# A graph layer on one core: the mixing branch's first product for two tiles at once, and five gather slots

## The reference

```python
xn = layernorm(x)
x = x + gnn(xn, edges) + mix(xn)          # gnn: softmax over each node's edges, weighted sum of rows
x = x + ffn(layernorm(x))                 # eight experts, three products each, gates by a softmax
# mix, per node:
h = relu(batchnorm(logmap0(xn) @ w_qkv))  # 256 -> 768 channels: the product of this change
s = w_pw(w_dw * h)                        # 768 -> 768, beside h itself
q, k, v = ...                             # 512 each, from cat(h, s)
out = relu(q) * sum(relu(k)) * v / (v + eps)   # per group of 32
mix = w_res(out) + b_res                  # with norms clipped in between
```

## Time and profile before

| | |
|---|---|
| median of 3 runs | 1184.98 us (1182.02 to 1188.89) |
| the profiled execution | 1176.66 us |
| its span | 1174.9 us |
| busy PE / DVE / ACT / POOL | 83% / 67% / 45% / 32% |
| PE passes (matmul records) | 5483, with as many weight loads |
| mean granted clock of PE | 0.923 |

### The profile page before, as it was taken

How to read it: one execution, slowest core, us unless ns; L and a number is a source line. 1 busy time by engine, 2 the same in 40 slices (tenths; PEclk the granted TensorE clock), 3 DMA queues, 4 the chain that set the end, 5 groups by cost and what they waited for, 6 DMA issues and landing times.

```text
span 1174.9 us, 15618 instructions
## 1 busy us (share of the span) xinstructions
PE 973.4 (83%) x5483; PEld 838.3 (71%) x5483; DVE 787.9 (67%) x1394; ACT 529.1 (45%) x1088; POOL 380.3 (32%) x408
## 2 busy tenths in 40 slices
PE   0998477878878888888764558999999999999996
PEld 0776356766767767766653447889978899998986
DVE  6786557777877977879787874676555454554544
ACT  1200034444444444444432135656655666667663
POOL 0034755666666666666676500000000000000000
PEclk9997779999998898999977777999999999999999
DMA  7332433434334343443447410000000000000012
GB/s 208 115 88 73 135 97 112 115 105 118 109 112 122 102 121 98 117 118 106 116 117 214 140 51 5 1 1 1 16 13 1 28 21 8 27 1 1 1 37 74
DMA packets 51375, 89.39 MB, mean 76 GB/s; under 512 B 10454, under 2 KB 34346, under 8 KB 51277
## 3 DMA queue, kind: packets, MB, share of 16 engines
q0 software_dynamic: 18768, 52.88, 16.6%
q1 hardware_dynamic: 32509, 35.27, 9.5%
HBM read 81.42 MB, written 6.68 MB: 75 GB/s over the span
## 4 chain that ended last, share of the span: by engine, by line
PE 55%; DVE 20%; issue 12%; ACT 6%; another core or an unknown queue 4%; DVEq 1%; DMA 1%; SPq 0%; ACTq 0%; POOL 0%; POOLq 0%
PE bank L872 12%; PE bank L873 11%; PE bank L874 11%; PE bank L750 5%; DVE U L1310 4%; DVE G L1202 3%; PE bank L788 3%; PE bank L680 2%; PE bank L709 2%; PE bank L799 2%; ACT junk L490 2%; PE bank L813 2%; DVE oh L1190 1%; PE bank L939 1%
## 5 line engine op out<-in xcount | busy, mean ns | idle before, releaser
L428 POOL DMA_INDIRECT G<-projected_rows,src_l x391 | 376.9, 964 | 288.9 <-issue 106.6
L750 PE MATMUL bank<-G,oh 128*128 128x264 f32 x782 | 201.9, 409 | 73.4 <-issue 38.9
L1473 DVE TENSOR_TENSOR hil<-hid,hil 128x1024 fp32r<-128x1024 f32 (+2 forms) x112 | 121.9, 1089 | 201.8 <-ACT hil L621 201.7
L750 PEld LDWEIGHTS bank<-G,oh 128*128 128x128 f32 x782 | 153.3, 201 | 111.4 <-issue 51.3
L613 ACT ACTIVATE hid<-bank,faff 128x512 f32<-128x512 f32 (+2 forms) x224 | 158.9, 722 | 151.6 <-PE bank L874 149.6
L872 PE MATMUL bank<-ew,hil 128*128 128x256 f32 (+1 forms) x400 | 113.5, 284 | 1.5 <-DVE feat_rows L1485 1.5
L873 PE MATMUL bank<-ew,hil 128*128 128x256 f32 (+1 forms) x400 | 113.0, 283 | 0.0
L874 PE MATMUL bank<-ew,hil 128*128 128x256 f32 (+1 forms) x400 | 113.0, 282 | 0.0
L621 ACT CAST hil<-hid 128x1024 fp32r<-128x1024 f32 (+2 forms) x112 | 105.3, 940 | 9.8 <-ACT hid L613 0.4
L1202 DVE TENSOR_TENSOR G<-G,bank 128x3072 f32<-128x3072 f32 (+1 forms) x33 | 109.0, 3304 | 0.0
L788 PEld LDWEIGHTS bank<-feat_rows,wqkv 128*128 128x128 f32 x600 | 82.6, 210 | 20.1 <-ACT TT L504 12.0
(11 more groups left out here) (289 smaller groups left out, 1656.4 us busy)
## 6 DMA issues: line engine op xcount, KB each, us to landing
dstb<-targets SPq DMA_DIRECT2D x32, 384.0 KB
G<-projected_rows,src_l POOLq DMA_INDIRECT x391
projected_rows<-sums SPq DMA_DIRECT2D x25, 132.0 KB, 3.6
x_in<-in_x SPq DMA_DIRECT2D x3, 1024.0 KB, 8.3
U<-in_x SPq DMA_DIRECT2D x24, 128.0 KB
out<-feat_rows SPq DMA_DIRECT2D x24, 128.0 KB
TT<-in_W SPq DMA_DIRECT2D x8, 256.0 KB
wqkv<-in_W SPq DMA_DIRECT2D x8, 256.0 KB
```

The source lines that it names most:

```text
L428: g.indirect_dma_start(out=G[slot][:, c, :], out_offset=None, in_=table[:, :], in_offset=bass.IndirectOffsetOnAxis(ap=src_l[:, grp, c:c + ...
L750: ins = T.matmul(b_seg[g % 2][:, 0:ROW], oh[g % 2][:, c, :], G[g % SLOTS][:, c, :], start=(c == 0), stop=(c == ch - 1))
L1473: V.tensor_tensor(hidl[layer][par][:, :, 0:cols], hid[layer][:, :, 0:cols], hidh[layer][par][:, :, 0:cols].bitcast(F32), ALU.subtract).the ...
```

## The change

The first product of the mixing branch is taken for a pair of tiles. A round is two chunks of 128 channels (4 matmuls of up to 256 columns) and fills `b_z`; three rounds make a pair, 13 pairs make 39 rounds (the last pair is one tile). Rounds are spread over two iterations: in an iteration with even t one early and one late round, with odd t only one early; in the iteration before tile 0 all three of the first pair, one early and two late. ACT normalises a round with two instructions of 256 columns and sets one semaphore, `z_evac`; the next round waits for it. u_rows takes its half of the pair's buffer. A pair's `TT` needs twice the columns of a tile; there are two such buffers, and the second one lies where the sixth gather slot was, so there are five slots.

```diff
-SLOTS = 6
+SLOTS = 5
+ROUNDS = 3 * -(-NT // 2)
...
+        tt_odd = sb("TT_odd", [P, EC * ROW])
...
-        TT = [tt_all[:, i * MC * P:(i + 1) * MC * P].rearrange("p (c n) -> p c n", c=MC) for i in range(2)]
+        TT = [b[:, 0:2 * MC * P].rearrange("p (c n) -> p c n", c=MC) for b in (tt_all, tt_odd)]
...
+        def rounds_of(t):
+
+            if t == -1:
+                return (0,), (1, 2)
+            first_ = 3 * (t // 2 + 1)
+            both = ((first_,), (first_ + 1,)) if t % 2 == 0 else ((first_ + 2,), ())
+            return tuple(tuple(r for r in slot if r < ROUNDS) for slot in both)
+
+        def round_of(r):
+
+            pair, part = divmod(r, 3)
+            start = 2 * pair * P
+            return pair, range(2 * part, 2 * part + 2), start, min(2 * P, NPAD - start)
...
-                    sp.wait_ge(s["zb_mm"], NT)
+                    sp.wait_ge(s["z_mm"], ROUNDS)
...
-            def batch_norm(t, chunks):
-                act.wait_ge(s["za_mm" if chunks[0] == 0 else "zb_mm"], t + 1)
-                for c in chunks:
-                    ins = A.activation(TT[t % 2][:, c, :], b_z[:, c % 4 * P:(c % 4 + 1) * P], ACT.Relu,
+            def batch_norm(r):
+                pair, chunks, _, cols = round_of(r)
+                act.wait_ge(s["z_mm"], r + 1)
+                for i, c in enumerate(chunks):
+                    ins = A.activation(TT[pair % 2][:, c, 0:cols], b_z[:, i * 256:i * 256 + cols], ACT.Relu,
                                        bias=baff[:, 1, c:c + 1], scale=baff[:, 0, c:c + 1])
-                ins.then_inc(s["bna_done" if chunks[0] == 0 else "tt_ready"], 1)
+                ins.then_inc(s["z_evac"], 1)
...
-            def channels(t, cs):
-                if cs[0] == 0:
+            def channels(r):
+                _, chunks, start, cols = round_of(r)
+                if r == 0:
                     pe.wait_ge(s["baff_ready"], 1)
-                    need(pe, s["tt_ready"], t)
-                    done = s["za_mm"]
-                else:
-                    pe.wait_ge(s["bna_done"], t + 1)
-                    done = s["zb_mm"]
-                for c in cs:
+                need(pe, s["z_evac"], r)
+                for i, c in enumerate(chunks):
                     for k in range(KC):
-                        ins = T.matmul(b_z[:, c % 4 * P:(c % 4 + 1) * P], wqkv[:, k, c * P:(c + 1) * P], FM[:, k, t * P:(t + 1) * P],
+                        ins = T.matmul(b_z[:, i * 256:i * 256 + cols], wqkv[:, k, c * P:(c + 1) * P], FM[:, k, start:start + cols],
                                        start=(k == 0), stop=(k == KC - 1))
-                ins.then_inc(done, 1)
+                ins.then_inc(s["z_mm"], 1)
 
             def u_rows(t):
-                pe.wait_ge(s["tt_ready"], t + 1)
+                pe.wait_ge(s["z_evac"], 3 * (t // 2 + 1))
...
-                        ins = T.matmul(bank[m][:, h * 256:(h + 1) * 256], TT[t % 2][:, c, :], ip[:, 0:c + 2:c + 1, :], start=True, stop=True)
+                        ins = T.matmul(bank[m][:, h * 256:(h + 1) * 256], TT[t // 2 % 2][:, c, t % 2 * P:(t % 2 + 1) * P], ip[:, 0:c + 2:c + 1, :], start=True, stop=True)
...
-                if 0 <= t + 1 < NT:
-                    channels(t + 1, range(0, 4))
+                early_rounds, late_rounds = rounds_of(t) if -1 <= t < NT else ((), ())
+                for r in early_rounds:
+                    channels(r)
```

More of the change, by code:

```diff
@@ L127, in program @@
             ew_all = late_sb("ew", 2 * 2 * 3 * KC * F)
-            late_sb("under_slots", SLOTS * EC * ROW - 2 * KC * NPAD - 2 * 2 * 3 * KC * F, F32)
+            late_sb("under_slots", (SLOTS + 1) * EC * ROW - 2 * KC * NPAD - 2 * 2 * 3 * KC * F, F32)
             hid_all = [late_sb(f"hid{i}", KC * MAXB, F32) for i in range(2)]
@@ L263, in program @@
             "sw_mm prod_ready var_mm baff_ready acc_init",
-            "za_mm zb_mm bna_done tt_ready u_mm u_evac fsq_ready qk_ready eps_ready",
+            "z_mm z_evac u_mm u_evac fsq_ready qk_ready eps_ready",
             "o_ready o_tr oT_ready r_mm mixed_ready no2_ready",
@@ L545, in _ @@
                     epsilon(t)
-                if 0 <= t + 1 < NT:
-                    batch_norm(t + 1, range(0, 4))
+                early_rounds, late_rounds = rounds_of(t) if -1 <= t < NT else ((), ())
+                for r in early_rounds:
+                    batch_norm(r)
                 if 0 <= t - 1 < NT:
                     mixed_out(t - 1)
-                if 0 <= t + 1 < NT:
-                    batch_norm(t + 1, range(4, MC))
+                for r in late_rounds:
+                    batch_norm(r)
                 if g == NA + MIX0 + 1:
@@ L838, in _ @@
                     mixed_out(t - 1)
-                if 0 <= t + 1 < NT:
-                    channels(t + 1, range(4, MC))
+                for r in late_rounds:
+                    channels(r)
             pe.wait_ge(s["mx_tr"], 1)
```

## The result

The change takes the kernel from 1183.5 us (median of 4, 1178.48 to 1188.89) to **1170.42 us** (median of 4, 1167.79 to 1172.42) on the same chip (the median of before has one run more than in the table ahead of the prediction). The ratio is 0.9889, its 95% interval 0.9852 to 0.9926: faster by 1.1%, 13 us. The forecast was 1164 us with a range of 1146 to 1198. The profiled execution took 1172.42 us (span 1170.5), against 1176.66 (1174.9) before.

The account below looks back on a forecast made before the run. In the main loop, PE stalls were taken to hold up DVE above its 16.2 us per iteration. Relief of 21 us and about 0 elsewhere took the profiled 1176.66 to about 1156, plus 8.3 to the median: 1164 us, range 1146 to 1198.

Parts of the forecast that it names:

- The bound and what there was to win: Main loop, 160 to 615 us: DVE's own 16.2 us per iteration is the bound; 41 us could be won.
- The excess of 41 us: DVE's wait at its once-per-tile reduction: 60.4 us, less 19.5 us that clean iterations have too.
- The gaps: -21 us: Main loop: fewer PE instructions relieve the stalls, -21 us, the middle between 5.7 and all 41.
- the proportional 5.7: Lower end of the main loop's relief: excess shrinks only with PE's instruction count, 0.14 x 41 = 5.7 us.
- The expected sign: Profile after: PE's "issue" before L750 and L813 well under 53 us.
- Array time, ACT, order: 0: Main loop: 2 us less array time, 20 us less ACT work and the new round order, each booked at 0.
- (d): Even iterations: the long late round meets the stall, slower, 1200 to 1212 us; 0.20 with weaker forms (1190 to 1212).
- The start: +4.5 - 4: Before tile 0: making the whole first pair loses 4.5 us, a shorter L750 crawl regains 4; about 0.
- (b): Main loop: relief only proportional, -5.7 + 4.5 - 2, about 1182 us; chance 0.13.
- the offset: Whole kernel: the median lies 8.3 us above the profiled execution, taking about 1156 to 1164 us.
- (a): PE's loop: gaps are the price of two branches between L750 and L813, which stay; 1187 us, chance 0.13.
- (c): Whole kernel: stalls belong to recording the profile and go from the profiled execution alone; timed 1187 us, chance 0.08.

Follow-up runs that it names:

- experiment 8: The kernel before with 6 of 12 gathers per group from the seventh group on: 1117.78 us and 1118.07 us, ratio 1.0 both times, on chips without gaps.
- experiment 4: The kernel before without PE's two branches and their register loads in each iteration: 1187.0 us, ratio 1.0006.
- experiment 1: The changed kernel, unaltered, on another chip: 1118.23 us against 1118.13 of the kernel before there, ratio 1.0002.

## Why the prediction held, point by point

**The bound and what there was to win.** Right. The reading of the clean iterations, 16.2 us under the gaps, is what the chips without gaps do in 17 of 24 intervals. The excess of 41 us was the right size too: on these chips the loop takes 43 us less (440.1 - 397.4, the second of after, since before has no profile there), and it was put down to the gaps. What makes the gaps it left open, and so do the runs.

**The gaps: -21 us.** Right in kind, near in size: the loop gave 18.7 in the two profiles. The value came from the middle between the proportional 5.7 and all 41, which is a choice and no working, so that it came so near is in part luck. That the count of instructions is behind it is supported by three loops: after with twelve small matmuls 441.8, after with the products split 437.1, after with one wide matmul 426.5. The expected sign, "issue" before L750 and L813 well under 53 us, came (3.5 us), but it was a bad sign: 28.3 us of it had moved to L757. PE's gaps in all fell by 12 us only, and DVE's idle time in the loop by 18.9. Why DVE gains more than PE's gaps lose is not worked out by any row; the gap at L757 ahead of the next group's score rows can lie beside DVE's own work, which fits, and was not tested.

**Array time, ACT, order: 0.** Right where there are no gaps: the 288 passes more of the split version cost nothing there. The array's time itself was sized low: in the two windows of experiment 8 PE is busy for 344.95 us with before's products and 339.47 with after's, 5.5 us and not 2. Where there are gaps, the split version's loop (437.1 against 445.9 on the same chip) leaves room for some us of the rounds and of ACT's steps, from one profile each. ACT's normalisations, 55.5 us for 144, are 72 of 35.9 us in after: 19.6 us less against 20 in the forecast, and no late step of an iteration was seen to wait for it. Rival (d), the long round that meets a stall, did not come as a whole: where L803 ran its 8 passes in one piece in the loop they took 1.89 or 1.99 us, and the intervals got shorter. In a few rounds gaps broke the eight up (6.7 us in 7 gaps).

**The start: +4.5 - 4.** Right in its sum and not in its path: the first reduction starts at 160.47 us, before at 160.48. Order of time in after, PE and ACT at tile 0:

```profile
121.47 1.97 PE L803 MATMUL bank<-feat_rows,wqkv 128*128 128x256 f32 x8
...
132.18 0.38 PE L768 MATMUL bank<-G,oh 128*128 128x264 f32 x1 [0.33 <-issue]
...
147.59 1.02 ACT L521 ACTIVATE TT<-bank,baff 128x256 f32<-128x256 f32 x2 [13.62 <-remote]
148.66 3.78 PE L803 MATMUL bank<-feat_rows,wqkv 128*128 128x256 f32 x8 [16.10 <-ACT TT L521]
...
153.55 1.99 PE L803 MATMUL bank<-feat_rows,wqkv 128*128 128x256 f32 x8 [1.11 <-ACT TT L521]
155.38 0.45 PE L757 MATMUL bank<-hsel,ohT 128*128 128x24 bf16 x12
```

From the late part to L757 it takes 155.38 - 148.66 = 6.7 us, before 152.80 - 150.93 = 1.87: 4.9 lost, inside the 4.3 to 6.1. Of these, 150.93 - 148.66 = 2.3 us come back ahead of it and the rest behind it. The crawl of L750 up to 150.93 is gone; PE has done with it at 132.56, 18 us earlier. But ACT then stands 13.62 us before the normalisation of a product that was ready at 121.47 + 1.97 us, and takes nearly all of it back. On chip 4 the same normalisation starts at 131.88 right behind the exponentials of 131.61, and the first reduction at 148.6. So that stand is no dependency of the program. It looks like the same disturbance on the next engine, and the relief of PE's crawl brought no more than 2.3 us.

**What the sum lacked: the rest after the last tile, +14.** The prediction priced the stretch from 160 to 615 us, and let the end move along with it. This is the term that it lacked: 14.3 of the 18.7 us gained in the loop were given back next to 17 unbroken gathers. After with the twelve small matmuls, where the loop gains nothing, has before's rest of 574.3 us. In total the change won 13 us by the medians, between the forecast's -21 and rival (b)'s -3.

**From the profiled execution to the median.** The sum was made at 1156 and set 8.3 us higher, as before's profiled execution stood under its median. After's stands 2.0 above (1172.42 and 1170.42). The miss by the sum is 1172.4 - 1156 = 16 us, of which 14.3 are the tail and 2.3 the smaller relief; the offset hid 10.3 of it. The 6 us between 1164 and 1170.42 are small because two errors oppose each other, which is luck. Two smaller slips: rivals (a) and (b) are priced with +4.5 for the start and -2 for the passes where the forecast books both at about 0, and the upper end of the range, 1198, is called the lower part of (d), which by its own sum begins at 1200.

**The rivals.** (a) was refuted by experiment 4. The Trainium skill, "Runtime: NRT & Kernel Launch", section "Instruction fetch mechanics", says that a taken branch whose target lies outside the prefetched pages stalls the engine for a fetch; in this kernel removing them from PE's loop changed nothing (1.0006), so here it was no part of the time. Whether these targets lie outside those pages no run here shows. (b) has the sign and not the size. (c), that the gaps are in the profiled execution alone, is refuted as it was put: the timed runs got faster by 1.1% where the profile shows gaps and by nothing where it shows none, and before is 65 us slower there in its timed runs too. In a wider form it stands, and it is the strongest rival left: every timed run here lists a span and a granted clock, as a recorded one does, and records of landings are missing just where the gaps are (experiment 1). If the gaps hang on recording, so do the 13 us. (d) did not happen.

**What stays open.** Which path backs up. That it clears when the gathers pause fits the tail (after 613.51, all engines go on at 616.71 to 617.75) and the start (the row of POOL's gathers ends at 143.28 us, ACT goes on at 147.59), but in no run on a chip with gaps were the gathers fewer. Fewer gathers would also mean fewer records of landings (6417 in place of 8923 on chip 4), so that run alone would not tell gathers from records; one that records nothing would. Why some chips show the gaps and others not is open too. And whether a pause in the tail could bring back the 14 us there: with its price of 13 us, hardly in the form tried. After itself was not run beside its variants on chips 8 and 10, so that its comparison with them may go across chips, and no version was faster than after on a chip with gaps.

## What to carry to other kernels

When several engines stand still together in mid-series, with "issue" or an unknown releaser, run the kernel on a second chip before anything is priced, and look whether the trace is whole: here that one look split the time into 1118 us that the kernel needs and 65 that came on some chips only, together with missing records, and showed that the change works on the second part alone. Merging narrow matmuls into wider ones seems to relieve such gaps through the number of instructions, and was worth nothing where another engine set the pace (1.0002). And a gain in one stage needs a line in the sum for the next stage: compare the time from the stage's last row to the end, before and after.

## What the runs showed of the hardware

- The same kernel takes 1118 us on two chips (2 and 4) and 1183 to 1187 us on others (8, 10 and that of the result), with the same instructions. Whether that is the chip or its surroundings at that time was not separated. The difference lies in the start (11.9 us), the loop (24.0 us for after; for before 42.7, if its loop on the other chips is the 397 that its version with half the gathers shows) and the tail (19.0 us for after).
- The gaps do not stay with a certain instruction: 22.4 and 30.6 us at L750 and L813 became 46.2 and 14.5 with the branches out, and 28.3 at L757 with the merged products.
- Beside 17 gathers in a row PE creeps on one kind of chip (24 passes of the sums take from 604.45 to 619.10 us) and not on the other: there gathers follow one another without a pause from 566.33 to beyond 590 us, and 24 passes of the same sums beside them take from 568.25 on 5.61 us. "Beside" is all that the rows show; that the gathers are the cause was not shown.
- Where the gaps are, the trace lacks records: 3260 to 3611 landings in the eight profiles with gaps, 8921 to 8930 in the four profiles without gaps that have all their gathers. Which of the two brings the other, or whether a third thing brings both, was not shown.
